# Two of four transposes of normalised x go from TensorE to VectorE block transposes and transfers, in a fused attention and mixture-of-experts kernel

## What is computed

```python
x = x + tanh(g_xattn[0]) * attention(layernorm(x), ctx, ctx, wq, wk, wv, wo)
x = x + tanh(g_ffn[0]) * experts(layernorm(x), shared_up, shared_down,
                                 routed_up, routed_down, router_w)
# attention: 16 heads of 64, rotary q and k, causal window of 64, softmax, output weights wo
# experts: 2 shared and 16 routed, 4 chosen per token; gelu between up and down
```

## Time and profile before

| | us |
|---|---|
| median of 3 runs | 523.23 |
| lowest and highest | 522.9, 523.24 |
| the profiled execution, its own time | 523.18 |
| span of its trace | 521.4 |
| PE busy in the span | 503.8 |
| DVE, ACT, POOL busy | 357.4, 311.1, 276.1 |
| attention stage in the trace, about | 10 to 305 |

### The profile page before, as it was taken

How to read it: one execution, slowest core, us unless ns; L and a number is a source line. 1 busy time by engine, 2 the same in 40 slices (tenths; PEclk the granted TensorE clock), 3 DMA queues, 4 the chain that set the end, 5 groups by cost and what they waited for, 6 DMA issues and landing times.

```text
span 521.4 us, 12294 instructions
## 1 busy us (share of the span) xinstructions
PE 503.8 (97%) x4394; PEld 422.2 (81%) x4394; DVE 357.4 (69%) x1150; ACT 311.1 (60%) x859; POOL 276.1 (53%) x213
## 2 busy tenths in 40 slices
PE   8888999899999999999999999999999999999996
PEld 4767798799889988888888888867887888788884
DVE  6868868558756577775967575697657665855463
ACT  3468677466676657766675794764546545544442
POOL 3989997788889778987998733541000100000000
PEclk9999999999999999999999999999999999999999
DMA  8352323111031011202221128314911491156021
GB/s 258 98 166 50 81 77 105 55 37 36 4 117 36 13 27 36 59 1 58 58 56 43 37 74 314 88 28 107 301 25 21 127 284 17 24 150 233 1 33 47
DMA packets 47723, 44.12 MB, mean 85 GB/s; under 512 B 29168, under 2 KB 31472, under 8 KB 47664
## 3 DMA queue, kind: packets, MB, share of 16 engines
q1 hardware_dynamic: 47664, 43.35, 29.2%
HBM read 30.62 MB, written 2.23 MB: 63 GB/s over the span
## 4 chain that ended last, share of the span: by engine, by line
PE 72%; POOL 10%; DVE 9%; issue 5%; ACT 2%; DMA 1%; SPq 0%; DVEq 0%; POOLq 0%; ACTq 0%
PE ring L1009 50%; PE psS L1009 8%; PE psO L1191 5%; PE psS L1160 4%; PE psT L1172 4%; POOL arena L465 3%; POOL arena L467 2%; POOL prob L471 2%; DVE arena L768 2%; POOL wl L479 1%; POOL arena L458 1%; DVE prob L819 1%; DMA craw<-in_ctx 1%; DVE wl L840 1%; DVE arena L910 1%
## 5 line engine op out<-in xcount | busy, mean ns | idle before, releaser
L1009 PE MATMUL ring<-xTh,wh 128*128 128x512 f32 x272 | 109.7, 403 | 3.0 <-DVE wl L840 1.4
L1009 PE MATMUL ring<-xTh,wl 128*128 128x512 f32 x272 | 106.8, 393 | 0.0
L1009 PE MATMUL ring<-xTl,wh 128*128 128x512 f32 x272 | 106.7, 392 | 0.0
L471 POOL TENSOR_TENSOR prob<-prob,rinv 128x512 f32<-128x512 f32 x64 | 68.0, 1063 | 15.5 <-DVE rinv L920 15.5
L566 ACT ACTIVATE oTh<-prob 128x512 fp32r<-128x512 f32 x64 | 40.4, 632 | 58.0 <-PE ring L1009 26.5
L827 DVE TENSOR_TENSOR oTl<-prob,oTh 128x512 fp32r<-128x512 f32 x64 | 46.3, 724 | 39.4 <-ACT oTh L566 39.1
L1009 PEld LDWEIGHTS ring<-xTh,wh 128*128 128x128 f32 x272 | 51.1, 188 | 16.6 <-issue 4.4
L819 DVE TENSOR_TENSOR prob<-sneg,arena 128x512 f32<-128x512 f32 x64 | 47.4, 740 | 21.6 <-ACT sneg L550 21.6
L637 ACT ACTIVATE pT<-psT 128x512 f32<-128x512 f32 x64 | 38.0, 593 | 40.3 <-PE psT L1172 40.3
L550 ACT ACTIVATE sneg<-ring 128x512 f32<-128x512 f32 x72 | 42.8, 595 | 32.0 <-PE ring L1009 31.9
L1009 PEld LDWEIGHTS ring<-xTh,wl 128*128 128x128 f32 x272 | 51.0, 188 | 11.3
(11 more groups left out here) (123 smaller groups left out, 1226.2 us busy)
## 6 DMA issues: line engine op xcount, KB each, us to landing
arena<-gate_scratch SPq DMA_DIRECT2D x64, 256.0 KB, 6.4
raw<-in_e SPq DMA_DIRECT2D x18, 256.0 KB, 2.7
raw<-in_w SPq DMA_DIRECT2D x16, 256.0 KB, 3.6
arena<-arena SPq DMA_DIRECT2D x16, 256.0 KB, 3.1
arena<-arena SPq DMA_DIRECT2D x16, 192.0 KB, 3.4
pT<-pT SPq DMA_DIRECT2D x96, 32.0 KB, 2.0
out<-x SPq DMA_DIRECT2D x16, 128.0 KB, 6.2
x<-in_x SPq DMA_DIRECT2D x3, 512.0 KB, 3.8
```

The lines of the kernel that those rows point to most:

```text
L471: pool.tensor_tensor(prob[:, c % BUFS, :, :], prob[:, c % BUFS, :, :], rinv[:, c % BUFS, :].unsqueeze(2).to_broadcast([P, TT, P]), ALU.mul ...
L1009: last = pe.matmul(out, a, b, start=start and i == 0 and j == 0, stop=stop and i == n - 1 and j == 2, skip_group_check=check)
```

## The change

The table `steps` treats batches 2 and 3 (the third and the fourth) differently; batch 1 keeps what it had (its four jobs stand in the same steps, under other conditions), and so do batch 0 and the feed-forward stage.

- For batches 2 and 3 the job `xT` is gone: 8 PE transposes, ACT's rounding out of PSUM, DVE's rest out of PSUM. It no longer takes a turn in `ring`.
- In its place DVE transposes `xn` in 32x32 blocks, one half of the features at a time, into the buffer `idle` (`turn_a`, `turn_b`); SP moves each half back into `xn` by 16 transfers (`move_half`); ACT rounds `xn` into `xTh[0]` in one instruction (`xhi_early`); DVE subtracts in two halves (in `xhi_early` and `xlo_early`).
- The jobs stand in these steps of the batch before: as (place k, group g) they are stat (0, 0), norm_a (1, 0), norm_b (2, 0), turn_a (3, 0), turn_b (2, 1), xhi_early (2, 2), xlo_early (3, 2). As numbers of the table that is c = 16, 17, 18, 19, 22, 26, 27 for batch 2, and 16 more for batch 3. Before they were c = 23 (stat), 24, 25 (norms) and 26 (xT), and 16 more.
- New jobs stand behind a step's q, k or v and ahead of its y.

```diff
--- before.py
+++ after.py
@@ -175,6 +175,7 @@
         gT_out, gT_dram = sem("gT_out"), sem("gT_dram")
         xn_turned, x1_turned = sem("xn_turned"), sem("x1_turned")
         xn_moved, x1_moved = sem("xn_moved"), sem("x1_moved")
+        half_turned, half_moved = sem("half_turned"), sem("half_moved")
         gate_in = [sem(f"gate_in{i}") for i in range(NR)]
         up_pe, f_gelu, f_mul = sem("up_pe"), sem("f_gelu"), sem("f_mul")
         f_hi, f_lo, down_pe = sem("f_hi"), sem("f_lo"), sem("down_pe")
@@ -202,10 +203,14 @@
                 jobs.append(("k", u + 1))
             if k == 2 and u + 1 < UNITS:
                 jobs.append(("v", u + 1))
-            if (k, g) == (2, 2) and b + 1 < B:
-                jobs.append(("xT", b + 1))
-            if (k, g) == (3, 1) and b + 1 < B:
-                jobs.append(("stat", b + 1))
+            early = {(0, 0): "stat", (1, 0): "norm_a", (2, 0): "norm_b", (3, 0): "turn_a", (2, 1): "turn_b",
+                     (2, 2): "xhi_early", (3, 2): "xlo_early"}
+            if 1 <= b < B - 1 and (k, g) in early:
+                jobs.append((early[k, g], b + 1))
+            if (c, b) == (G + 3, 0):
+                jobs.append(("stat", 1))
+            if c == 2 * G + 2:
+                jobs.append(("xT", 1))
             if c == CHUNKS - 13:
                 jobs.append(("stat", B))
             if k == 3:
@@ -214,10 +219,8 @@
                 jobs.append(("ctx", b + 1))
             if c in WEIGHT_STEPS:
                 jobs.append(("w", WEIGHT_STEPS[c]))
-            if (k, g) == (0, 2) and b + 1 < B:
-                jobs.append(("norm_a", b + 1))
-            if (k, g) == (1, 2) and b + 1 < B:
-                jobs.append(("norm_b", b + 1))
+            if c in (2 * G, 2 * G + 1):
+                jobs.append(("norm_a" if c == 2 * G else "norm_b", 1))
             jobs += {CHUNKS - 12: [("norm_a", B)], CHUNKS - 11: [("norm_b", B)], CHUNKS - 5: [("xT", B)]}.get(c, [])
             steps.append((c, jobs))
 
@@ -292,6 +295,10 @@
 
             return u // 2 + 1
 
+        def by_pe(j):
+
+            return j if j < 2 else j - B + 2
+
         def side(j):
 
             return 0 if j < B else (j - B) % 2
@@ -355,6 +362,15 @@
                     for c in range(4):
                         to = dst[QUAD * c:QUAD * (c + 1), :].rearrange("p (m a j) -> p m a j", m=KC * TT, a=4)
                         sp.dma_start(to[:, :, a, :], mine[:, :, c, :]).then_inc(done, 16)
+
+            def move_half(half):
+
+                cols = slice(half * P, half * P + P)
+                for a in range(4):
+                    mine = idle[QUAD * a:QUAD * (a + 1), :].rearrange("p (t c j) -> p t c j", t=TT, c=4)
+                    for c in range(4):
+                        to = xn[QUAD * c:QUAD * (c + 1), :, cols].rearrange("p t (a j) -> p t a j", a=4)
+                        sp.dma_start(to[:, :, a, :], mine[:, :, c, :]).then_inc(half_moved, 16)
 
             def spread_gates(n):
 
@@ -409,6 +425,10 @@
                     shift_values(n)
                 elif kind == "spread":
                     spread_gates(n)
+                elif kind in ("turn_a", "turn_b"):
+                    half = kind == "turn_b"
+                    sp.wait_ge(half_turned, 2 * (n - 2) + half + 1)
+                    move_half(half)
                 elif kind == "turn":
                     sp.wait_ge(xn_turned, n - 1)
                     move(x1_blocks, xn_blocks, xn_moved)
@@ -532,7 +552,7 @@
         def _(act):
 
             def round_bank_pair(dst, job, ready, done):
-                act.wait_ge(ready, job[1] + 1)
+                act.wait_ge(ready, by_pe(job[1]) + 1)
                 two = banks(job)
                 if job in ring_at:
                     act.activation(dst[:, :, :], both_banks(job)[:, :, :], ACT.Copy).then_inc(done, 1)
@@ -606,13 +626,23 @@
                     act.wait_ge(up_pe, NE * (n - 1))
                     act.wait_ge(r_pe, n - 1)
                     act.activation(xTh[X][:, :, :], xnT, ACT.Copy).then_inc(xT_hi, 1)
+                elif kind == "xhi_early":
+                    act.wait_ge(half_moved, 512 * (n - 1))
+                    act.wait_ge(qk_pe[0], rotated("q", GROUPS * n - 1))
+                    act.activation(xTh[0][:, :, :].rearrange("p k (t c) -> p k t c", t=TT),
+                                   xn[:, :, :].rearrange("p t (k c) -> p k t c", k=KC), ACT.Copy).then_inc(xT_hi, 1)
                 elif kind in ("norm_a", "norm_b"):
                     normalise(n, kind)
 
             def normalise(j, kind):
                 act.wait_ge(ln_rstd, j + 1)
-                act.wait_ge(xT_pe, min(j, B + 2))
-                if j > B + 2:
+                if j <= 2:
+                    act.wait_ge(xT_pe, j)
+                elif j <= B:
+                    act.wait_ge(xT_lo, j)
+                elif j <= B + 2:
+                    act.wait_ge(xT_pe, j - B + 2)
+                else:
                     act.wait_ge(xn_turned, j - B - 2)
                 for t in range(TT // 2) if kind == "norm_a" else range(TT // 2, TT):
                     last = act.activation(xn[:, t, :], x[:, j % B, t, :], ACT.Identity,
@@ -870,6 +900,22 @@
                     for a in range(4):
                         last = dve.transpose(by_tokens[:, :, a, :], gate[QUAD * a:QUAD * (a + 1), :, :])
                     last.then_inc(gT_out, 1)
+                elif kind in ("turn_a", "turn_b"):
+                    half = kind == "turn_b"
+                    dve.wait_ge(ln_norm, n + 1)
+                    if n > 2 or half:
+                        dve.wait_ge(half_moved, 256 * (2 * (n - 2) + half))
+                    dve.transpose(idle.rearrange("p (t c) -> p t c", t=TT),
+                                  xn[:, :, half * P:half * P + P]).then_inc(half_turned, 1)
+                elif kind in ("xhi_early", "xlo_early"):
+                    kc = 0 if kind == "xhi_early" else 1
+                    dve.wait_ge(xT_hi, n + 1)
+                    rest = dve.tensor_tensor(xTl[0][:, kc, :].rearrange("p (t c) -> p t c", t=TT),
+                                             xn[:, :, kc * P:kc * P + P],
+                                             xTh[0][:, kc, :].rearrange("p (t c) -> p t c", t=TT).bitcast(F32),
+                                             ALU.subtract)
+                    if kc:
+                        rest.then_inc(xT_lo, 1)
                 elif kind == "turn":
                     dve.wait_ge(ln_norm, B + n + 1)
                     dve.wait_ge(z_out, 4 * (n - 1))
```

## The result

| | before | changed |
|---|---|---|
| median, us | 523.07 (4 runs) | 530.67 (4 runs, 530.32 to 531.34) |
| the profiled execution | 523.18 | 530.74 |
| span of its trace | 521.4 | 528.9 |
| mean granted TensorE clock | 0.999 | 0.993 |

The ratio is 1.0147, with a 95% interval of 1.0132 to 1.0162: slower by 7.6 us. The forecast was 528.0 us, with a range of 526.0 to 531.5.

A forecast was written before the change was run, and what follows sets the result against it. TensorE, busy 503.8 of 521.4 us, was taken as the bound. 523.18 - 2.01 (removed) + 6.86 (moved `stat`) + 0 (added) = 528.03, so 528.0 us; own range 527.0 to 529.9, 8 in 10 for 526.0 to 531.5.

The forecast's parts named there:

- The bound and the slack: TensorE bounds the kernel; in step 35 the late divisions end 1.21 and 0.90 us before TensorE's transposes would wait.
- The moved `stat`: Steps 16 and 32: GpSimd's queue comes 4.33 us later, idling PE 3.43 us per unit, 6.86 us in all.
- 2.09 over 2.59 us for the statistics: VectorE's statistics in step 32: 2.09 us beside an idle GpSimd, 2.59 beside a busy one; 2.09 was taken.
- What is removed from PE: Transposes gone ahead of y in steps 27 and 43: saves 0.93 and 1.08 us, together 2.01 us.
- the next one late: Batch 3, y without its wait for v's copy: the rest of the value sums holds y until about 215.53.
- What is added: VectorE's block transposes, 0.62 us each, SP's transfers and the split subtractions: nothing on the path; 2.5 us if uncovered.
- The term for a GpSimd slowed by the transposes: GpSimd slowed beside the first block transpose of each batch: 0 to 0.9 us in all, taken as 0.
- rival 1: Clock falls to 1.2 GHz behind TensorE's two pauses, doubling y's 2.96 us: one drop 531.0, two 533.9 us; chance 0.14.
- GpSimd's wait wasn't hidden: Rival that GpSimd's wait for the moved statistics is hidden and the kernel is faster: 521.2 us; chance 0.06.
- no transfer was waited for: Rival that SP's transfers come late and hold VectorE's second block transpose: some 7 us in all, 535 us; chance 0.04.
- the pauses weren't shorter than read: Rival that the moved wait costs half, each TensorE pause some 1.5 us shorter: 525.0 us; chance 0.08.

## Why the prediction was right

**The bound and the slack**: right. The saving is real, and the stretch had 1.21 and 0.90 us of slack in front of PE, as read. The pause forecast as 3.12 us is 3.15 from start to start.

**The moved `stat`**: right to a tenth. Statistics 2.09 forecast, 2.08 measured; q's rotation on GpSimd later by 4.33 us forecast. In the trace after, with VectorE's q rotation as common mark, it starts 180.44 - 175.91 = 4.53 us behind the cosine product. In the kernel before (timeline of DVE):

```profile
172.26 1.21 DVE L771 TENSOR_TENSOR arena<-ring,cos 128x1024 f32<-128x1024 f32 x1
```

There it was 172.45 - 172.26 = 0.19, so q's rotation comes 4.34 us later. With the clock held up, two such places cost 6.87 us; forecast 6.86. The choice of 2.09 over 2.59 us for the statistics was right for the reason given. The run that put the same small row beside a busy GpSimd shows that I hadn't read what stood behind the earlier trace rows: the upper end isn't 0.50 us but what is left of the GpSimd instruction, 1.9 us there.

**What is removed from PE**: 2.01 us forecast, 1.93 measured. PE around steps 27 and 43 of the changed kernel:

```profile
147.82 0.60 PE L1218 MATMUL psT<-ident,prob 128*128 128x128 f32 x4
148.17 0.37 PE L1055 MATMUL ring<-wh,oTh 128*128 128x256 f32 x1
...
223.17 0.60 PE L1218 MATMUL psT<-ident,prob 128*128 128x128 f32 x4
223.98 0.36 PE L1055 MATMUL ring<-wh,oTh 128*128 128x256 f32 x1 [0.21 <-DVE oTl L970]
```

y follows the transposes after 0.35 us, as in step 35, and after 0.81 us, behind a wait of 0.21 for the rest of the value sums. v's copy no longer holds it, and the next one late was named rightly; it was sized 0.08 us too small, as from VectorE's end to PE's start it is 0.15 us and not the 0.05 taken over from a signal of GpSimd.

**What is added**: rightly costed at nothing. Rows of the changed kernel's trace, and two of its instruction groups.

Timeline of SP, steps 35 to 38:

```profile
186.86 11.16 SPq L373 DMA_DIRECT2D xn<-arena  x16
206.79 0.51 SPq L354 DMA_DIRECT2D arena<-arena  x1
```

DVE's block transposes, then its subtractions (ns min/median/max, first and last start):

```profile
L908 DVE STREAM_TRANSPOSE arena<-xn x4: 698/705/711, 110.7 to 205.1; 128x512 f32<-128x512 f32 x4
...
L913 DVE TENSOR_TENSOR xTl<-xn,xTh x4: 692/1199/1685, 150.0 to 226.6; 128x512 fp32r<-128x512 f32 x4
```

A half's 16 transfers keep SP for 11.2 us and are done before the next shift of v at 206.79. The estimate of 0.62 us for the transpose of a half was short, it takes 0.70. The one of step 35 started at 186.12; as v in that step starts 3.65 us later in this trace (180.21 against 176.56), that is 182.5 in the times of before, where I had put it. The term for a GpSimd slowed by the transposes, 0 to 0.9 us in the prediction, came out at 0: its division and its rotation beside the one at 186.12 took 1.04 and 1.28 us, as elsewhere. The second subtraction of each pair took 1.68 or 1.69 us instead of 0.7, and the GpSimd rotations beside the last one 1.78 and 1.62 instead of 1.28; no run isolates the cause. Nobody waited for them.

**The step that failed is the weight of rival 1.** The clock did fall, behind both pauses, and I gave that 0.14; the sum itself had it at nothing. The 530.67 us lie above the forecast's own range of 527.0 to 529.9, and inside 526.0 to 531.5 only because that was stretched to take in one fall at a price that was too high. Its price was oversized: I doubled the whole y product, 2.96 us each, and took that on top. It came out at 1.2 us each, as the product was only partly at the lower clock (1.57 us longer) and 0.3 us of it replaced the wait for the second division. With the measured sizes rival 1 with both falls gives 528.0 + 2.4 = 530.4, and this is what happened. So the time is the forecast's chain plus the rival's clock. The rule of the Trainium skill that the prediction quotes ("TensorE: Matmul & The Clock Gate", Why this matters for your kernels), no idle gaps over about 3 us or the clock goes back to half, fits the pauses of 3.00 and 3.01 us. The trace also has the fall behind one of 2.31 us, which is shorter; ahead of that one stood only four transposes, 2.90 us from their start to y's. And the fourth run with only the statistics moved kept a mean clock of 1.000.

**The other rivals** didn't come: GpSimd's wait wasn't hidden (5.65 us), no transfer was waited for, and the pauses weren't shorter than read.

## What to carry to other kernels

Before moving a small job to another step, ask what is queued behind its wait on each engine, and compare the delay with the slack of what those instructions feed; here a job of 2 us of VectorE and 1.25 us of GpSimd, in two places, cost 9.3 us in all (530.67 - 521.38), and moving it ahead of one rotation turned the loss into a gain. A pause of a few microseconds on a busy TensorE is to be costed with the clock behind it, 1.2 us each here. When a change can save 2 us at most, try by itself first the part of it that merely moves a job to another place.

## What the runs showed of the hardware

- A pause of TensorE of 3.0 us in otherwise full work was followed by 3 to 4 us at the 1.2 GHz level, twice in the trace of the changed kernel; the mean clock was 0.992 or 0.993 in all of its four runs, and under 1.000 in three of four of a kernel with the same pause. One of 2.31 us behind four transposes was followed by it too. The waits of 1.45 and 1.32 us in the kernel before weren't: the granted clock stays at 1.00 around both.
- Filling the pause with 1.9 us of unneeded matmuls, so that 1.29 us of idle time remained, kept the clock at 1.00.
- The first VectorE `tensor_scalar` of 128x4 behind the statistics took 0.17 us beside an idle GpSimd and 0.51 to 2.09 us beside a busy one (traces of the kernel before and of the run with only VectorE's part moved), and ended each time within 0.03 us of a GpSimd instruction. The statistics rows beside it weren't lengthened (1.38 to 1.40 us for four, beside a busy and an idle GpSimd).
